# Routing the last six batches of a decoder layer as one group, with their gate exponentials as powers on GpSimd

## The reference, cut to what matters

```python
x = layernorm(x + attn(x))            # softmax over head features and over tokens, a 16x16 state per head
x = layernorm(x + xattn(x, ctx))      # 16 heads, softmax over 128 context rows
g = gelu(x @ wg1 + bg1); probs = softmax(g @ wg2)          # 8 experts
top_vals, top_idx = top_k(probs, 2)
h = gelu(x @ w_in[e]); o = h @ w_out[e]                    # 256 -> 512 -> 256 per expert
x = layernorm(x + sum over the two chosen e of top_vals * o[e])
```

## Time and profile before

| | |
|---|---|
| runs | 430.15 us median of 3 (430.11 to 433.9) |
| profiled execution | 431.93 us, of which its span is 430.1 us |
| TensorE | 347.9 us busy, 81% of the span |
| VectorE, ScalarE, GpSimd | 308.3, 222.1 and 220.7 us busy |
| mean granted TensorE clock | 0.923 |

### The profile page before, as it was taken

One profiled execution on the slowest core, in us unless ns is written; L12 is line 12 of the kernel. 1 busy time (PEld: TensorE's weight loads), 2 busy tenths in 40 slices (PEclk: granted clock), 3 DMA queues, 4 the chain that ended last, 5 costly groups with the idle time before them and its releaser, 6 DMA issues. The chain is left out here.

```text
span 430.1 us, 12345 instructions
## 1 busy us (share of the span) xinstructions
PE 347.9 (81%) x4025; PEld 281.0 (65%) x4025; DVE 308.3 (72%) x912; ACT 222.1 (52%) x518; POOL 220.7 (51%) x287
## 2 busy tenths in 40 slices
PE   2977999999999999999887185759999999999200
PEld 1655777777777877777664053547899999988100
DVE  3767899888988889888777077468677666755193
ACT  3435676667666676766763045353544444444034
POOL 8335456676666766667258554643133333422273
PEclk9999999999999999999898588569999999999855
DMA  7520022220122211221012222325525322321393
GB/s 219 179 76 27 2 75 75 75 77 21 56 75 77 75 39 38 76 75 50 2 53 100 87 77 79 109 76 151 156 81 155 84 69 61 98 75 39 124 378 122
DMA packets 21387, 38.35 MB, mean 89 GB/s; under 512 B 3696, under 2 KB 11120, under 8 KB 21328
## 3 DMA queue, kind: packets, MB, share of 16 engines
q1 hardware_dynamic: 16768, 26.06, 19.8%
q0 software_dynamic: 3408, 9.41, 6.1%
q10 hardware_dynamic: 1152, 2.10, 1.3%
HBM read 24.71 MB, written 12.84 MB: 87 GB/s over the span
## 5 line engine op out<-in xcount | busy, mean ns | idle before, releaser
L575 POOL DMA_INDIRECT parts<-QKT,rows_all x39 | 37.8, 969 | 76.1 <-DVE QKT L1207 65.9
L328 PE MATMUL bank<-QS,EW 128*128 128x256 f16 (+1 forms) x384 | 62.6, 265 | 5.6 <-DVE XB L1021 5.6
L491 POOL TENSOR_TENSOR rstd<-veps,neghalf 128x1 f32<-128x1 f32 x48 | 39.6, 824 | 41.6 <-DVE veps L844 41.2
L1382 PE MATMUL bank<-EW,QV 128*128 x312 | 48.7, 273 | 1.8 <-DVE R L1199 0.8
L328 PE MATMUL bank<-XB,EW 128*128 128x256 f16 (+1 forms) x192 | 49.0, 264 | 0.0
L1199 DVE TENSOR_TENSOR R<-scratch,QV 128x512 f16<-128x512 f32 x39 | 26.7, 691 | 29.4 <-ACT scratch L764 17.9
L1126 DVE TENSOR_REDUCE NM<-bank 128x4 bf16<-128x512 f32 x64 | 39.6, 678 | 11.1 <-remote 10.1
L328 PEld LDWEIGHTS bank<-QS,EW 128*128 x384 | 37.7, 102 | 11.6 <-issue 6.1
L764 ACT ACTIVATE scratch<-bank 128x512 f32<-128x512 f32 x39 | 23.4, 600 | 40.5 <-PE bank L328 38.5
L506 POOL DMA_INDIRECT bkt<-REC,dest x32 | 32.9, 1029 | 21.3 <-issue 11.9
L699 ACT ACTIVATE rows_all<-bank 128x512 f32<-128x512 f32 x64 | 33.2, 603 | 18.2 <-remote 10.8
(11 more groups left out here) (240 smaller groups left out, 941.4 us busy)
## 6 DMA issues: line engine op xcount, KB each, us to landing
scratch<-w_in SPq DMA_DIRECT2D x8, 512.0 KB, 3.3
scratch<-w_out SPq DMA_DIRECT2D x8, 512.0 KB, 3.8
rows_all<-bkt SPq DMA_DIRECT2D x15, 262.0 KB
XC<-x SPq DMA_DIRECT2D x16, 128.0 KB, 3.3
XC<-ctx SPq DMA_DIRECT2D x16, 128.0 KB, 3.2
EW<-parts SPq DMA_DIRECT2D x8, 256.0 KB, 6.8
EW<-parts ACTq DMA_DIRECT2D x8, 256.0 KB, 7.4
out<-rows_all SPq DMA_DIRECT2D x8, 256.0 KB, 2.1
```

What stands on the lines that cost most here:

```text
L328: last = pe.matmul(dst, a(c), b(c), start=(c == 0 and i == 0), stop=(c == n - 1 and i == 2))
L491: pool.tensor_tensor(rstd[n][p][:], veps[n][p][:], neghalf[:, 0:1], ALU.pow).then_inc(s_rs[n], 1)
L575: pool.indirect_dma_start(parts, bass.IndirectOffsetOnAxis(ap=home[:, t, f:f + 1], axis=0), Y[t % 2][:, f, :], None).then_inc(s_put[t % 2] ...
L1382: last = pe.matmul(bank[4 + t % 2][:, f * D:(f + 1) * D], a[t % 2][:, h, f * P:(f + 1) * P], b[:, h, :], start=(h == 0 and i == 0 and f == 0),
```

## The change

The last six batches become one group: one Gelu over three pairs, one `lg`, one pair of choices, one count, 12 scatters together. `exps` and `second` of that group move from ScalarE to GpSimd, as powers of e, ahead of the 12 scatters. The third group's steps are gone from every engine; ScalarE loads the Gelu table once (`hot:0`), and has no exponential after that. In the tails the order changes: `pw1:15` stands ahead of all scatters, `x1b:15` behind `sc:3`, `pw2:12` behind `sc:5`, `pw2:13` behind `sc:11`, `pw2:14` behind `sc:16`; VectorE's `n1:15` moves up, `full:1`, `full:2` move ahead of `O2T:14` and `ewl:15`, and `low:0` stands ahead of `choice1:1`. TensorE turns tile 0 before the late `lg`, and does the first `up` in two halves with the count and `turn:1` between.

```diff
-EDGE = (0, EARLY, 14, NB)
+EDGE = (0, EARLY, NB)
...
+            pool.memset(euler[:], float(np.exp(1.0))).then_inc(s_cst, 1)
...
+                if step == "exps":
+                    pool.wait_ge(s_off, b + 1)
+                    rows = slice(EDGE[b], EDGE[b + 1])
+                    n = EDGE[b + 1] - EDGE[b]
+                    pool.tensor_tensor(LE[:, rows, :].rearrange("p b e -> p (b e)"), euler[:].to_broadcast([P, n * NE]),
+                                       L[:, rows, :].rearrange("p b e -> p (b e)"), ALU.pow).then_inc(s_le, 1)
+                if step == "second":
+                    pool.wait_ge(s_gap, b + 1)
+                    rows = slice(EDGE[b], EDGE[b + 1])
+                    pool.tensor_tensor(second[:, rows], euler[:].to_broadcast([P, EDGE[b + 1] - EDGE[b]]), gap[:, rows], ALU.pow)\
+                        .then_inc(s_second, 1)
...
-                     "sc:0 sc:1 pw1:15 sc:2 sc:3 sc:4 sc:5 sc:6 sc:7 sc:8 pw2:12 sc:9 sc:10 sc:11 sc:12 sc:13 sc:14 pw2:13 "
-                     "sc:15 sc:16 x1b:15 sc:17 pw2:14 sc:18 sc:19 pw2:15 "
-                     "sc:20 sc:21 sc:22 sc:23 sc:24 sc:25 sc:26 sc:27 sc:28 sc:29 sc:30 sc:31")
+                     "pw1:15 sc:0 sc:1 sc:2 sc:3 x1b:15 sc:4 sc:5 pw2:12 sc:6 sc:7 sc:8 sc:9 sc:10 sc:11 pw2:13 sc:12 sc:13 sc:14 sc:15 sc:16 "
+                     "pw2:14 sc:17 sc:18 sc:19 pw2:15 "
+                     "exps:1 second:1 sc:20 sc:21 sc:22 sc:23 sc:24 sc:25 sc:26 sc:27 sc:28 sc:29 sc:30 sc:31")
...
+                if step == "hot":
+                    act.preload_act_table(ACT.Gelu)
...
-                     "lns:15 rec:15 X2T:13 gcp:13 gelu:1 X2T:14 exps:1 X2T:15 second:1 gcp:15 gelu:2 high:0 "
-                     "exps:2 second:2 high:1")
-            act.preload_act_table(ACT.Gelu)
+                     "lns:15 rec:15 hot:0 X2T:13 gcp:13 X2T:14 X2T:15 gcp:15 gelu:1 high:0 high:1")
...
-                     "mx0:14 mx1:14 n1:15 mx2:14 mx3:14 R2:12 s2:12 full:0 O2T:13 nr:13 full:1 QM1:15 full:2 mx0:15 mx1:15 mx2:15 "
-                     "R2:13 n2:12 mx3:15 s2:13 ewl:15 O2T:14 nr:14 ewl:16 R2:14 n2:13 s2:14 ewl:17 O2T:15 nr:15 n2:14 R2:15 s2:15 "
-                     "choice1:1 n2:15 choice2:1 gate1:1 dest:1 gate2:1 "
-                     "choice1:2 low:0 choice2:2 whose:0 gate1:2 dest:2 gate2:2 low:1 whose:1")
+                     "mx0:14 n1:15 mx1:14 mx2:14 mx3:14 R2:12 s2:12 O2T:13 nr:13 QM1:15 full:0 n2:12 mx0:15 mx1:15 mx2:15 "
+                     "mx3:15 R2:13 s2:13 full:1 O2T:14 nr:14 full:2 n2:13 ewl:15 ewl:16 R2:14 s2:14 ewl:17 O2T:15 nr:15 R2:15 s2:15 n2:14 "
+                     "n2:15 low:0 choice1:1 choice2:1 gate1:1 dest:1 gate2:1 whose:0 low:1 whose:1")
...
-                if step == "up":
+                if step == "upa":
                     pe.wait_ge(s_tables, 1)
                     pe.wait_ge(s_ewl, 2 * NE)
                     held[b] = expert_of(b)
-                    up(b, held[b])
+                    up(b, held[b], range(0, HC // 2))
+                if step == "upb":
+                    up(b, held[b], range(HC // 2, HC))
...
-                     "x2T:13 cntpre:1 gh:13 ao2:15 x2T:14 lg:1 x2T:15 gh:15 cnt:1 lg:2 turn:0 cntpre:2 up:0 turn:1 cnt:2")
+                     "x2T:13 cntpre:1 gh:13 ao2:15 x2T:14 x2T:15 gh:15 turn:0 lg:1 upa:0 cnt:1 turn:1 upb:0")
```

More of the change, by code:

```diff
@@ L95, in decoder_layer @@
         neghalf = sb("neghalf", [P, NB])
+        euler = sb("euler", [P, 1])
         rowb = sb("rowb", [P, NROW])
@@ L300, in decoder_layer @@
         NAT_BANK, SC_BANK = (0, 7, 6, 5), (2, 1, 4, 3)
-        LGP = [bank[(7, 5, 5)[g]][:, 0:(EDGE[g + 1] - EDGE[g]) * NE] for g in range(NG)]
-        PLP = [bank[(6, 4, 4)[g]][:, 256:256 + (EDGE[g + 1] - EDGE[g] + 1) * NE] for g in range(NG)]
+        LGP = [bank[(7, 5)[g]][:, 0:(EDGE[g + 1] - EDGE[g]) * NE] for g in range(NG)]
+        PLP = [bank[(6, 4)[g]][:, 256:256 + (EDGE[g + 1] - EDGE[g] + 1) * NE] for g in range(NG)]
         def group(b):
@@ L451, in _ @@
                 pool.memset(V2[p][:], 0.0).then_inc(s_cst, 1)
-            pool.wait_ge(s_cst, 11)
+            pool.wait_ge(s_cst, 12)
             for t in (ident, identb):
@@ L480, in _ @@
             pool.iota(spare_i[:], [[TW, MAXT], [P, HALVES]], base=0, channel_multiplier=1).then_inc(s_cst, 1)
-            pool.wait_ge(s_cst, 18)
+            pool.wait_ge(s_cst, 19)
             pool.affine_select(out=before[:], in_=before[:], compare_op=ALU.is_ge, fill=0.0, base=-1,
@@ L1354, in expert_of, with up @@
                 return pe.value_load(texp[0:1, t:t + 1], min_val=0, max_val=NE - 1)
-            def up(t, e):
+            def up(t, e, hs=range(HC)):
                 pe.wait_ge(s_tTl, t + 1)
@@ L1364, in up @@
                 wi_h, wi_l = (EW_v[:, e, lo, 0, :].rearrange("p (k h) -> p k h", k=KC) for lo in range(2))
-                for h in range(HC):
+                for h in hs:
                     last = split3(pe, bank[2 * (t % 2) + h // hc][:, h % hc * n * P:(h % hc + 1) * n * P],
@@ L1368, in up @@
                                   lambda c: TXh[t % 2][:, c, 0:n * P], lambda c: TXl[t % 2][:, c, 0:n * P])
-                last.then_inc(s_up, 1)
+                if HC - 1 in hs:
+                    last.then_inc(s_up, 1)
             def down(t, e):
```

## The result

The kernel after takes 442.63 us (median of 4, 441.88 to 443.46), the kernel before beside it 432.02 (430.11 to 435.27): ratio 1.0247, 95% interval 1.019 to 1.0305. It is slower, as forecast, but by more: the 442.63 lies 5.6 us above the forecast and 0.6 above the top of the range. Of the 5.6, 1.9 are the kernel before itself, whose median is 432.02 here where the forecast started from 430.15. The profiled execution took 441.88 us with a span of 439.2, against 431.93 and 430.1.

The account below looks back on a forecast made before the run. Bound: tile 3's turn on TensorE (296.89 us) plus an unchanged remainder. The first `up` 4.0 us earlier, but the turn 4.4 later at 301.3, plus 2.5 for the clock: +6.9, so the median goes from 430.15 to 437.0; range 426 to 442.

Parts of the forecast that it names:

- The failed step: Early tail: the first `up` was to start at 269.4 us, 4.0 earlier than before (bounds 9 earlier to 1 later).
- The release: Early tail: TensorE's held signals reach the other engines at 244.0 us, 2.4 earlier, as GpSimd pauses behind 12 scatters, not 15.
- the 25.4: Early tail: time in us from the release to the first `up`, 27.0 before, less a net 1.6.
- the hold: During GpSimd's scatters: a long unbroken series holds TensorE's signals until it pauses, from some 8 to 10 us in.
- The removals: Ahead of the first `up`: a table load of 1.28 us, the choice chain and a second Gelu's waiting go, saving at most 4.0.
- U: The start of the first `up`, from which the late part is counted; forecast at 269.4 us, 273.38 before.
- the late part: From U to tile 3's turn: powers of 7.4 and 1.3 us, then 12 scatters; U + 31.9, where it was U + 23.5.
- the second rival: Late scatters: the series of 12 holds TensorE's signals from U + 20 on, catching rounds 1 and 2; chance 0.1.
- the clock: At tile 3's turn: TensorE comes out of an idle stretch at a lower clock, adding 2.5 us (0 to 3.5).
- Cheap power: Late exponentials on GpSimd: the 48-element power is short, gates at U + 5, 431.5 us in all; chance 0.2.
- Longer holds: Early and late scatters: early pause falls at `pw2:14`, U no earlier, late series holds signals; 441 to 443 us, chance 0.1.
- No early hold: Early scatters: the new order ends the early hold, U at 262, turn at 294, 430 us (424 with cheap power); chance 0.2.

Follow-up runs that it names:

- h4: The kernel after with twelve further plain writes issued by GpSimd behind the late scatters, on chip 3: 433.83 us, one run.
- c1: The kernel after with the early GpSimd and VectorE lists of the kernel before, so one late group and powers alone: 440.44 us, ratio 1.019.
- b1: The kernel before with only the new early order of GpSimd and VectorE, on chip 12: 434.57 us, ratio 1.007.
- b2: The kernel before with only the new early order of GpSimd and VectorE, on chip 5: 435.34 us, ratio 1.006.
- h2: The kernel after with its twelve late scatters issued again at 24 bytes a row into an unread buffer, on chip 3: 440.44 us, one run.
- h1: The kernel after with each of its twelve late scatters issued once more into an unread buffer, on chip 12: 464.55 us, one run.
- p2: The kernel before with three pauses (powers of 12 elements) in GpSimd's early scatter series, on chip 11: 429.54 us, ratio 0.994.
- f1: The kernel before with its 20 early scatters spread between the powers in GpSimd's list, on chip 11: 427.29 us, ratio 0.988.
- p1: The kernel before with three pauses (powers of 12 elements) in GpSimd's early scatter series, on chip 3: 423.37 us, ratio 1.019.

## Why the prediction was right or wrong

**The failed step: "The first `up` then starts at 244.0 + 25.4 = 269.4, 4.0 us earlier than before".** The release came at 240.65, earlier than my 244.0. It was the 25.4 from there that failed: it took 33.1. I took this stretch over from the kernel before, less a net 1.6, as if it held no wait. But there it stood behind a long wait of 10.77 us, during which GpSimd got 15 of the 20 scatters out. Released earlier, behind 12, GpSimd issues five in a row next, and TensorE and ScalarE are caught once more (5.50 us). Ending a wait sooner did not end what causes it. I had the hold begin "some 8 to 10 us into the series", and of the 4-scatter series I had written that it "held nothing"; here TensorE stood 2.8 us into a series of five. And where no wait is (h4), the stretch takes 30.2: the new VectorE order puts `ewl:15`, and so the last weight load, 4.4 us later behind the release. I had named that step and priced it within the net gain of 1.6, without following it to `lns:15`. The removals, priced at 4.0 us at most, gave some 2.0 (c1's U). The early order, which I had at about nothing on balance (the release 2.4 us sooner, 2.3 us of `full:1` behind it), costs 2.4 us at U (c1 against the kernel after) and 3.1 of the time by itself (b1, b2).

**Right: the late part.** The power of 48 was 8.02 us for 7.4, the one of 6 was 1.33 for 1.3; the bound by the plain operations was far off. The gates were ready at U + 11.8 for U + 11, the series took 15.4 for 14.9, and the turn came 5.3 us behind it for 5.15; together these make the turn U + 33.3 for U + 31.9. c1 shows that this part alone makes 1.9%. The late hold was there, as the second rival had it (ScalarE until 303.70), and cost this trace 0.2 us at most: tile 3's load went out at 304.00, 2.3 us behind the last scatter as forecast, and TensorE, busy without a break from 303.48, came to the turn 3.06 us later, for 2.86. On chip 5 the same stretch was 4.2 us (305.57 to 309.78), so there the held work did set the turn. **Wrong: the clock.** I added 2.5 us behind the turn for TensorE coming cold to it. But TensorE came out of the hold at 303 with work to do, ran it at a granted clock of 0.50 until 307, and was at 1.00 from 308 on; the low clock lies ahead of the turn, inside U + 33.3. Behind the turn there are 132.1 us, against 133.2 before. Why these 1.1 fewer isn't shown.

In spans: the forecast +6.9; U +4.3 over the forecast, U to turn +1.4, the clock and the rest -3.6: +9.0, for a measured 439.2 - 430.1 = 9.1. So the early tail is the largest error, and the clock's hid most of it: by spans the forecast was only 2.2 us short, and that is luck. The other 3.4 of the 5.6 us are the base, 1.9 higher, and the medians, 10.6 us apart where the two spans are 9.1 apart. The range was missed by 0.6 us, so without any one of these errors upward the time would have been inside it, with the early tail read just as wrongly.

**The rivals.** Cheap power: refuted by the row of 8.02 us. Longer holds: U was not earlier, and the late series held; its 441 to 443 has the time, but by luck, since the early pause did not fall at `pw2:14` as it had it and the late hold moved the turn by 0.2 us. No early hold: refuted on four chips, and met on chip 3, where U was at 260.14 to 262.10 and h2's turn at 295.07, for its 262 and 294. I had put the Trainium skill's rule under it, "SBUF — State Buffer", section "Who interferes with whom", by which TensorE and ScalarE wait on no one for SBUF and DMA doesn't contend with the compute engines. On chip 3 the traces agree with it (h2: 35.7 us of scatters and puts in one series and no such wait); on the others TensorE is 3.42 us busy of 17 during h1's series. So as a forecast for this kernel it held on one chip of five. Where the waits arise no run shows, so they don't say that the rule itself is wrong.

**What is shown and what isn't.** Shown: on the chips with the waits, a longer series lengthens them (h1: 29.63 us, one run), and pauses or spreading shorten them (p2, f1). Shown too: the powers cost 5 to 7 us, the late part nearly the whole 2%, and the early order 3.1. Open: what in a series does it (issue, descriptors or bytes), since h2 to h4 met a chip without them; why one chip has none; and whether the third wait would have been replaced in full by the wait for the last weight load, since the kernel after with `ewl:15` alone put back wasn't run.

## What to carry to other kernels

A stretch read off a trace behind a long stall is not a plain duration: much of its work was done during the stall, so ending the stall sooner lengthens the stretch. When steps are reordered, follow each one that frees a buffer to the transfer that waits for it and on to the engine's next step. And on a queue that issues many small DMAs, put the steps that others wait for between them in short groups: that alone was worth 1.2% on a chip with the waits, more than anything in the change, though nothing on top of the change, and no run shows it on the chip without them.

## What the hardware showed beyond the forecast

GpSimd's power costs 0.56 us for one element a partition, 1.33 for 6, 2.31 for 12 and 8.02 for 48: near 0.16 us for each element more. ScalarE's two exponentials of before, 0.2 us each and a table load of 1.28, were far cheaper.

The same kernel takes 431 to 432 us on four chips and 415 on a fifth, where it wasn't traced. In the kernel that was traced on both kinds (p1, p2), 7.15 of 7.4 us lie ahead of tile 3's turn, where the waits during GpSimd's series of indirect DMAs are. A gain or loss that works through such waits holds for the chips that have them: the pauses lose 1.9% on the one and win 0.6% on another.
